# One handover for each 128-column block of the hidden layer instead of two, over six PSUM banks, in the expert stages

## The reference, cut to what matters

```python
h = jax.nn.relu(jnp.einsum('ebnc,ech->ebnh', buf, W1) + b1[:, None, None, :])
y = jnp.einsum('ebnh,ehc->ebnc', h, W2) + b2[:, None, None, :]
y_tok = y[e_flat, b_idx, pos_c]
y_tok = y_tok * keep[..., None].astype(x.dtype) * p_flat[..., None]
out = y_tok.reshape(B, T, K, C).sum(axis=2)
```

## Time and profile before

| | us |
|---|---|
| three runs | 3105.36, 3100.03, 3111.36 |
| median | 3105.36 |
| span of the profiled execution (first to last instruction) | 3008.1 |
| TensorE busy in it | 2783.3 (93%) |
| VectorE busy | 2329.8 (77%) |
| GpSimd busy | 2187.8 (73%) |
| ScalarE busy | 1803.2 (60%) |

### The profile page before, as it was taken

The page is one execution under the profiler, slowest core; times in us unless marked ns, Lnnn a source line. Parts: engine busy times, 40 slices in busy tenths (PEclk is TensorE's granted clock), DMA queues, the critical chain, the costliest instruction groups (busy, mean ns, idle before and its releaser), DMA issues. The chain is left out here.

```text
span 3008.1 us, 54043 instructions
## 1 busy us (share of the span) xinstructions
PE 2783.3 (93%) x16944; PEld 2226.0 (74%) x16944; DVE 2329.8 (77%) x4122; ACT 1803.2 (60%) x3430; POOL 2187.8 (73%) x1437
## 2 busy tenths in 40 slices
PE   6999989989989899899985899999899997999998
PEld 3566656566656566666664799999899997999998
DVE  4899998989989999899998667575567776666665
ACT  4766776667657766677663545454456664454553
POOL 4888998898989889989987665665335557565654
PEclk8999999999999999999998899999999997999999
DMA  6222221121112211221125454544333334454542
GB/s 169 74 103 73 87 73 40 62 88 71 46 59 87 74 44 59 88 73 44 52 80 205 128 117 115 118 118 115 68 103 116 116 130 130 113 125 112 126 111 36
DMA packets 192665, 281.66 MB, mean 94 GB/s; under 512 B 35943, under 2 KB 164622, under 8 KB 184264
## 3 DMA queue, kind: packets, MB, share of 16 engines
q1 hardware_dynamic: 157128, 236.31, 23.7%
q0 software_dynamic: 35328, 42.76, 7.9%
HBM read 197.28 MB, written 94.72 MB: 97 GB/s over the span
## 5 line engine op out<-in xcount | busy, mean ns | idle before, releaser
L550 POOL TENSOR_TENSOR dbu<-du,bb 128x1024 f32<-128x1024 f32 x512 | 1196.3, 2361 | 30.0 <-DVE hs L703 26.7
L703 DVE TENSOR_TENSOR_SCAN hs<-da,dbu 128x1024 f32<-128x1024 f32 x512 | 1150.7, 2279 | 81.0 <-ACT da L638 39.8
L638 ACT ACTIVATE da<-delta 128x512 f32<-128x512 f32 x1024 | 566.4, 594 | 239.0 <-DVE hs L703 228.6
L808 PEld LDWEIGHTS yT<-ident,hs 128*128 128x128 f32 x4096 | 482.8, 146 | 151.6 <-issue 85.8
L808 PE MATMUL yT<-ident,hs 128*128 128x128 f32 x4096 | 542.5, 282 | 19.7 <-DVE hs L703 19.7
L1371 POOL TENSOR_TENSOR ffn_w_lo<-ffn_w,ffn_w_hi 128x512 fp32r<-128x512 f32 x240 | 323.8, 1377 | 93.8 <-ACT ffn_w_hi L1366 93.8
L1451 PE MATMUL ffn_ybank<-ffn_w_hi,ffn_hT_hi 128*128 128x256 f32 x1280 | 367.2, 287 | 0.6 <-DVE ffn_hT_lo L1439 0.6
L1453 PE MATMUL ffn_ybank<-ffn_w_hi,ffn_hT_lo 128*128 128x256 f32 x1280 | 360.6, 282 | 0.0
L1452 PE MATMUL ffn_ybank<-ffn_w_lo,ffn_hT_hi 128*128 128x256 f32 x1280 | 359.8, 281 | 0.0
L1417 PE MATMUL ffn_hbank<-ffn_rowsT_hi,ffn_w_hi 128*128 128x320 f32 x1024 | 339.0, 331 | 3.3 <-POOL ffn_w_lo L1371 3.3
L1428 ACT ACTIVATE ffn_hT_hi<-ffn_hbank,ffn_b 128x320 fp32r<-128x320 f32 x512 | 269.2, 526 | 113.0 <-PE ffn_hbank L1419 113.0
(11 more groups left out here) (257 smaller groups left out, 4962.2 us busy)
## 6 DMA issues: line engine op xcount, KB each, us to landing
bb<-b_rows SPq DMA_DIRECT2D x64, 1024.0 KB, 4.6
ffn_w<-L_ffn_W SPq DMA_DIRECT2D x60, 1024.0 KB, 5.8
slots<-empty SPq DMA_DIRECT2D x40, 530.0 KB, 9.1
empty<-slots SPq DMA_DIRECT2D x16, 662.5 KB, 4.8
ffn_rows<-slots SPq DMA_DIRECT2D x16, 662.5 KB, 4.9
xt<-L_attn_a_x SPq DMA_DIRECT2D x16, 512.0 KB, 4.0
x<-L_attn_a_x SPq DMA_DIRECT2D x16, 512.0 KB, 4.0
x_after_mamba<-x SPq DMA_DIRECT2D x16, 512.0 KB, 2.9
```

The costliest lines, as they stand in the source:

```text
L550: pool.tensor_tensor(dbu[:, s % DEEP], du[:, dt, :].unsqueeze(1).to_broadcast([P, SN, T]), bb[:, q * SN:(q + 1) * SN, :], ALU.mult).then_i ...
L638: ins = act.activation(da[:, s % 2, i, :], delta[:, par, dt, :], ACT.Exp, scale=-float(q * SN + i + 1))
L703: dve.tensor_tensor_scan(flat[0], flat[1], flat[2], 0.0, ALU.mult, ALU.add).then_inc(scanned.sem, 1)
L808: mm = pe.matmul(yT[:, j * P:(j + 1) * P], hs[:, s % DEEP, i, j * P:(j + 1) * P], k.ident[:], start=False, stop=(q == QS - 1 and i == SN - ...
```

## The change

The handover between the two products is made once for a whole block (two banks, 640 rows) and not once for each job (one bank, 320 rows). `hbank` grows to six banks, three pairs that the blocks take in turn (`HB` = 3); `ybank` becomes its last two banks, so that the blocks 2 and 5 of the first product and the output tiles of the second product share them. The matmuls are the same, in the same order. ScalarE's ReLU and both of VectorE's instructions take both banks of the pair at once, with an access pattern of 2 by 320. TensorE now waits before a block (from block 3) for the block three before it, and two waits are new: block 2 waits for the last output tile of the turn before to be copied out, and the first output tile waits for block 5 to be split before it starts.

```diff
+        HB = 3
-        hbank = ctx.enter_context(nc.psum_tensor(name + "_hbank", [P, 4, 512], F32))
-        ybank = ctx.enter_context(nc.psum_tensor(name + "_ybank", [P, 2, 512], F32))
+        hbank = ctx.enter_context(nc.psum_tensor(name + "_hbank", [P, HN * HB, 512], F32))
+        ybank = hbank[:, HN * (HB - 1):, :]
-        h_mm, h_hi = Count(sem("h_mm"), NH * HN), Count(sem("h_hi"), NH * HN)
-        h_full, h_lo = Count(sem("h_full"), NH * HN), Count(sem("h_lo"), NH * HN, ahead=1)
+        h_mm, h_hi = Count(sem("h_mm"), NH), Count(sem("h_hi"), NH)
+        h_full, h_lo = Count(sem("h_full"), NH), Count(sem("h_lo"), NH)
...
         def first_product(pe, turn, par):
             for m in range(NH):
+                if m == 0:
+                    pe.wait_ge(t_lo.sem, t_lo.at(turn, TJ))
+                    pe.wait_ge(w_lo.sem, w_lo.at(turn, WP))
+                if m == HB - 1:
+                    pe.wait_ge(y_part.sem, y_part.at(turn - 1, NR))
+                if m >= HB:
+                    pe.wait_ge(h_lo.sem, h_lo.at(turn, m - HB + 1))
                 for n in range(HN):
-                    job = m * HN + n
-                    if job == 0:
-                        pe.wait_ge(t_lo.sem, t_lo.at(turn, TJ))
-                        pe.wait_ge(w_lo.sem, w_lo.at(turn, WP))
-                    pe.wait_ge(h_lo.sem, h_lo.at(turn, job - 3))
+                    bank = hbank[:, m % HB * HN + n, 0:HW]
...
-                    mm.then_inc(h_mm.sem, 1)
+                mm.then_inc(h_mm.sem, 1)
+
+        def hidden_banks(m):
+            return hbank[:, m % HB * HN:(m % HB + 1) * HN, 0:HW]
+
+        def hidden_part(t, m):
+            return t[:, m, :].rearrange("p (n t) -> p n t", n=HN)

         def relu(act, turn, par, m):

-            for n in range(HN):
-                job = m * HN + n
-                act.wait_ge(h_mm.sem, h_mm.at(turn, job + 1))
-                act.activation(hT_hi[:, m, n * HW:(n + 1) * HW], hbank[:, job % 4, 0:HW], ACT.Relu,
-                               bias=b1[:, par, m:m + 1]).then_inc(h_hi.sem, 1)
+            act.wait_ge(h_mm.sem, h_mm.at(turn, m + 1))
+            act.activation(hidden_part(hT_hi, m), hidden_banks(m), ACT.Relu, bias=b1[:, par, m:m + 1]).then_inc(h_hi.sem, 1)

         def split_hidden(dve, turn, par, m):

-            for n in range(HN):
-                job = m * HN + n
-                bank, at = hbank[:, job % 4, 0:HW], slice(n * HW, (n + 1) * HW)
-                dve.wait_ge(h_hi.sem, h_hi.at(turn, job + 1))
-                dve.tensor_scalar(bank, bank, b1[:, par, m:m + 1], 0.0, ALU.add, ALU.max).then_inc(h_full.sem, 1)
-                dve.wait_ge(h_full.sem, h_full.at(turn, job + 1))
-                dve.tensor_tensor(hT_lo[:, m, at], bank, hT_hi[:, m, at].bitcast(F32),
-                                  ALU.subtract).then_inc(h_lo.sem, 1)
+            banks = hidden_banks(m)
+            dve.wait_ge(h_hi.sem, h_hi.at(turn, m + 1))
+            dve.tensor_scalar(banks, banks, b1[:, par, m:m + 1], 0.0, ALU.add, ALU.max).then_inc(h_full.sem, 1)
+            dve.wait_ge(h_full.sem, h_full.at(turn, m + 1))
+            dve.tensor_tensor(hidden_part(hT_lo, m), banks, hidden_part(hT_hi, m).bitcast(F32), ALU.subtract).then_inc(h_lo.sem, 1)

         def second_product(pe, turn, par, parts):
...
                 for m in range(NH):
-                    if r == 0:
-                        pe.wait_ge(h_lo.sem, h_lo.at(turn, HN * (m + 1)))
+                    if r == 0 and m == 0:
+                        pe.wait_ge(h_lo.sem, h_lo.at(turn, NH - HB + 1))
+                    if r == 0 and m > NH - HB:
+                        pe.wait_ge(h_lo.sem, h_lo.at(turn, m + 1))
...
-                h_lo.grant(dve)
```

More of the change, by code:

```diff
@@ L1415, in first_product @@
+                if m >= HB:
+                    pe.wait_ge(h_lo.sem, h_lo.at(turn, m - HB + 1))
+                for n in range(HN):
+                    bank = hbank[:, m % HB * HN + n, 0:HW]
                     for c in range(NC):
                         ws, rs = slice(m * P, (m + 1) * P), slice(n * HW, (n + 1) * HW)
-                        pe.matmul(hbank[:, job % 4, 0:HW], w1_hi[:, par, c, ws], rowsT_hi[:, c, rs], start=(c == 0), stop=False)
-                        pe.matmul(hbank[:, job % 4, 0:HW], w1_hi[:, par, c, ws], rowsT_lo[:, c, rs], start=False, stop=False)
@@ L1419, in first_product @@
-                        mm = pe.matmul(hbank[:, job % 4, 0:HW], w1_lo[:, par, c, ws], rowsT_hi[:, c, rs], start=False,
-                                       stop=(c == NC - 1))
-                    mm.then_inc(h_mm.sem, 1)
-        def relu(act, turn, par, m):
-            for n in range(HN):
-                job = m * HN + n
-                act.wait_ge(h_mm.sem, h_mm.at(turn, job + 1))
-                act.activation(hT_hi[:, m, n * HW:(n + 1) * HW], hbank[:, job % 4, 0:HW], ACT.Relu,
-                               bias=b1[:, par, m:m + 1]).then_inc(h_hi.sem, 1)
@@ L1431, in split_hidden @@
-        def split_hidden(dve, turn, par, m):
-            for n in range(HN):
-                job = m * HN + n
-                bank, at = hbank[:, job % 4, 0:HW], slice(n * HW, (n + 1) * HW)
-                dve.wait_ge(h_hi.sem, h_hi.at(turn, job + 1))
-                dve.tensor_scalar(bank, bank, b1[:, par, m:m + 1], 0.0, ALU.add, ALU.max).then_inc(h_full.sem, 1)
-                dve.wait_ge(h_full.sem, h_full.at(turn, job + 1))
-                dve.tensor_tensor(hT_lo[:, m, at], bank, hT_hi[:, m, at].bitcast(F32),
-                                  ALU.subtract).then_inc(h_lo.sem, 1)
+                        pe.matmul(bank, w1_hi[:, par, c, ws], rowsT_hi[:, c, rs], start=(c == 0), stop=False)
@@ new lines, in first_product @@
+                        pe.matmul(bank, w1_hi[:, par, c, ws], rowsT_lo[:, c, rs], start=False, stop=False)
+                        mm = pe.matmul(bank, w1_lo[:, par, c, ws], rowsT_hi[:, c, rs], start=False, stop=(c == NC - 1))
+                mm.then_inc(h_mm.sem, 1)
[3 more added lines that the diff above has]
+            return t[:, m, :].rearrange("p (n t) -> p n t", n=HN)
+        def relu(act, turn, par, m):
+            act.wait_ge(h_mm.sem, h_mm.at(turn, m + 1))
+            act.activation(hidden_part(hT_hi, m), hidden_banks(m), ACT.Relu, bias=b1[:, par, m:m + 1]).then_inc(h_hi.sem, 1)
```

## The result

| | before | after |
|---|---|---|
| runs | 3105.36, 3100.03, 3111.36, 3093.69 | 3061.74, 3068.25, 3072.23, 3068.26 |
| median, us | 3102.70 | 3068.26 |
| ratio after / before, 95% interval | | 0.9895 [0.9871, 0.9919] |
| profiled execution: span | 3008.1 | 3059.9 |

The change makes the kernel faster, by 34 us where 21 were forecast. One thing doesn't fit at first sight: the changed kernel's profiled execution has a span 52 us longer than that of before, with fewer instructions in it.

A forecast was written before the change was run, and what follows sets the result against it. TensorE was taken to bound the kernel, stalled by VectorE's pace in the first product of the expert turns. Removing 21 us of stalls gave 3105.4 - 21 = 3084 us, range 3078 to 3098.

The forecast's parts named there:

- The mechanism: First product of expert turns: VectorE's 1.00 us a job against TensorE's 0.88 stalls TensorE; inner turns 30.26 to 29.58 us.
- the stall term: First against second matmuls of a split product, whole kernel: 339.0 - 318.1 = 20.9 us of stalls, all to go.
- VectorE's pair: Bias-and-maximum and subtraction over a whole block in the first product: near 0.88 and 0.82 us.
- Room at block 3: First product: block 0's banks free at 4.66 us, TensorE comes at 5.28; slack 0.62 us.
- Room at block 7: First output tile, second product: block 7 split at 16.98 us, wanted at 17.49; slack 0.5 us.
- VectorE's block of 1.66: First product: VectorE needs 1.66 us a block, below TensorE's 1.76, so it no longer sets the pace.
- The larger instructions are not too long: Rival, VectorE in the first product: larger instructions save little and turns lengthen, 3140 us; chance 0.07.
- The stall doesn't move: Rival: the stall reappears in the first output tile, gain partly or wholly gone, 3090 to 3108 us; chance 0.11.
- The shared banks expose nothing: Rival, banks shared by both products: the copy out is exposed, 0.67 us a turn at most, 3105 us; chance 0.04.
- the halves of the start turns: First turn of each expert stage: starts at half clock, stalls rarer, so that part of the 21 us is uncertain.
- the price: Stalls in expert stages: 21.8 us by 32 turns, 20.9 by matmul groups; 21 taken, also as the most.
- the 97.3 us: Whole kernel: the timed median's excess over the profiled span of 3008.1 us, carried over unchanged to the forecast.

The follow-up runs named there:

- single_six_banks: Kernel before with six banks, two shared with the output tiles, but still jobs of one bank (320 elements): 3095.57 us, ratio 0.9965 to the kernel before.
- pairs_four_banks: Kernel after with whole-block instructions on only four banks (two pairs) and output tiles in their own two banks: 3192.21 us, ratio 1.0279 to the kernel before.
- group 3: Runs on one quick chip: kernel before 3010.07 us; against the kernel after, scatters spread between weight pieces 2988.21, second-layer scatters writing one slot only 2985.55.
- before_again: The kernel before, unchanged, run and profiled again: 3106.31 us, ratio 0.9998 to itself.
- after_again: The kernel after, unchanged, run and profiled again: 3084.14 us, ratio 0.9930 to the kernel before.
- groups 1, 2 and 4: Three sets of follow-up runs, each on one chip with its own runs of the kernel before: 3105.49, 3094.95 and 3104.44 us.

## Why the prediction came out as it did

**The mechanism, right and to size.** TensorE was held at VectorE's pace in the first product, and the change ends that: an inner turn is 29.56 us for 29.58 forecast, the stall term 0.6 us for 0. VectorE's pair was put at 880 and 820 ns and takes 893 and 825; the ReLU at 800 and takes 796. Room at block 3: 1804.47 - 1803.73 - 0.1 = 0.64 us for 0.62. Room at block 7: 1816.66 - 1816.04 - 0.1 = 0.5 for 0.5. VectorE's block of 1.66 is seen where no ReLU holds it: 0.92 from bias to subtraction, and 1815.96 - 1815.22 = 0.74 from there to the next instruction.

**The rivals.** The larger instructions are not too long (1.66, where trouble starts at 1.81). The stall doesn't move: in an inner turn the first output tile has its step of 0.12 throughout. That this was a real rival is shown by single_six_banks, where it does move, at 0.39 us a turn. The shared banks expose nothing, with 1802.70 - 1799.85 = 2.85 us of room. On the rule of the Trainium skill that the prediction weighed (Perfetto Trace Analysis, section Optimizing Tensor Performance: independent matmul groups should rotate through different banks so that a copy overlaps the next group): it names the right danger, and this case doesn't break it, because the groups that meet in a shared bank are not neighbours. pairs_four_banks shows what it costs when the rotation is too short.

**The step that failed.** It is in the sum: "The median of the runs shown lies 97.3 above the span, and I carry that over: 3105.4 - 21 = 3084 us", with "Of the 21, only the halves of the start turns are soft", and in the price, where 21 us is called "also the most that the change can give". I took the 97.3 us for something outside the span that no part of the kernel sees. They lie inside: a profile's own time is its span and 1.8 us. The span of 3008.1 was of an execution about 95 us faster than those timed, and the 95 us are in two places, the attention stage (348 to about 430) and the first turn of each expert stage (31.7 to 38.0). So the second place is one that the change touches, in a state that the profile didn't show, and 21 us was the most only for the stalls of that one execution. Where no signal is late the forecast difference did come out, 22 us by the spans of group 3.

By turns, before_again against after and after_again, the change gives:

| | us |
|---|---|
| 28 inner turns, 847.0 to 827.8 | 19.2 |
| turns 15 and 31, 72.5 to 71.0 | 1.5 |
| turns 0 and 16, 76.0 to 69.4 and 69.8 | 6.4 |
| sum | 27 |

The first two lines are the 21 of the forecast. The third is the missing term, 6.4 us. A good part of it is the clock. With the granted shares of the stretches, before_again gives up 0.13 x 38.06 + 0.10 x 37.98 = 8.7 us in its two first turns and the kernel after 0.05 x 34.70 + 0.08 x 34.73 = 4.5, so up to 4 of the 6.4 us; it is an estimate from above, since TensorE stands still for a part of the slow stretches anyway. The other part goes with TensorE's idle time, 3.9 and 4.2 us in before_again against 2.5 and 1.9 in the kernel after.

Why the signals' lateness costs less after the change is argued and not isolated: a block waits for one late signal instead of two, and TensorE has six banks instead of four to run ahead into. single_six_banks, with the lead alone, has first turns of 36.5 and 36.6 us, and pairs_four_banks 36.7 and 38.5, with long stalls of its own; in both the clock falls a second time in turn 16. So both lie between 38.0 and 34.8, as if each half gave a part; but one profile each, with 1.4 us between first turns of the same code, can't divide the 3.2.

**Why 34 and not 27.** Outside the attention stage the four profiles of the kernel after have 2644.0, 2646.3, 2642.4 and 2645.9 us of span. The attention stage, which the change doesn't touch, has 415.9, 439.0, 414.1 and 443.0. With their mean of 2644.6, and 2673.1 for the kernel before (3102.9 - 429.8), the medians of a group, less the 1.8 us, give its length in both kernels: 427.8 and 421.8 us in the first measurement, then 430.6 and 437.7, 420.1 and 420.5, 429.5 and 432.3. The differences, after less before, are -6.0, +7.1, +0.4 and +2.8, their mean 1 us. All these are estimates, since they take the remainder from one profile of the kernel before and four of the kernel after. By them the first measurement, with four runs of each, had 6 us of luck. The four measurements give 34.4, 21.4, 28.0 and 25.7 us, on average 27, which is what the turns add up to. Even with the missing term the forecast would have been 3078; the width of the range had to come from the attention stage, and I had added 4 us, for the spread of three runs.

**What stays open.** Why the attention stage is 66 to 95 us longer on three of the four chips, and whether late signals make it so. Waits of the kernel after there that have grown most (engine and line waited for; us in total, times, longest):

```profile
POOL a_r_norm_rstd L139 <- DVE a_r_norm_away L133: 107.2, 16, 12.4
...
ACT a_prT L1859 <- remote: 34.2, 10, 4.9
...
PE a_ring L1921 <- issue: 25.5, 11, 4.4
```

In the prediction's profile the same GpSimd instruction waits 36.3 us in all and the same ScalarE instruction 4.7, 0.6 at most. "remote" says that the profile found no instruction whose end fits the signal, as a late signal from TensorE would look; which of the waits bounds the stage isn't shown. The scatters' data and the loads' place were tried, one run each, and neither brought the stage near 348 us. Group 3 differs from the others by more than either, but each group had one chip and one time: whether it is the chip, its place or its neighbours isn't known.

## What to carry to other kernels

A producer's lead in banks and the consumer's time per block are two levers, and they have to be checked together. More banks alone move a stall to where the lead ends; larger instructions alone shorten the lead, and the wait for a full block can cost more than the stall did. Before a forecast, hold the profiled span against the timed runs: if they are further apart than the 2 us that an execution adds, the profile isn't of the executions that will be compared, and a range has to allow for stages that it shows at their best. GpSimd's indirect DMAs are better spread between other instructions than issued in a row beside a burst of loads: on a chip with late signals that took 7 us off the two first turns, and on the one without it cost nothing that the runs can tell (2988.2 us against 2985.6 with the scatters in a row, intervals overlapping).

## What the runs showed of the hardware

- An instruction of VectorE or ScalarE over two banks costs what its elements cost: from 320 to 640 elements VectorE's bias and maximum goes from 550 ns (mean of 512 in the kernel before) to 893, its subtraction from 491 to 825, ScalarE's ReLU from 526 to 796: 1.07, 1.04 and 0.84 ns an element. Within one bank it was 1.03 on VectorE and 0.84 on ScalarE: the step to the next bank adds some 0.01 us at most.
- In groups 1, 2 and 4 the semaphore increment of a finished matmul came late in the first turns (up to 5.3 us in turn 0 of before_again) while the DMA engines were all busy (363 GB/s in before_again); in the prediction's profile, at 380 GB/s, and in group 3 it didn't. In the first turn the lateness goes with eight scatters 1.3 us apart beside loads: with the scatters moved to turn 1 it is there, and with one ahead of each weight piece, 2.5 us apart, it is gone.
- A TensorE that is held up can lose its clock as well: in before_again it was busy for 1.15 and 1.27 us of 3 from 1690 to 1696 us, and its granted clock was 0.50 from 1694.2 to 1701.0.
- The same kernel takes 3010 us on one chip and 3095 to 3105 on three others, and most of that is in one stage, 348 us in the kernel before on the first, and 414 to 443 us in all kernels on the others.
